# A fused two-block layer on one core, under another table of priorities for the orders of its engines

## The chip, the cores and the metric

The kernel runs on one core of one Trainium2 chip. The metric is the device time of one execution in microseconds, from launch to the last output in memory; the less, the better.

## What is computed

An input x of 2 x 1024 x 128 goes through four residual steps, each on the layer norm of x:

```python
x = x + attn_a(layernorm(x))   # three 128x128 projections, a linear recurrence over 1024 tokens, norm, projection
x = x + ffn(layernorm(x))      # 8 experts, all of them for every token, weighed
x = x + attn_b(layernorm(x))   # three MLPs, low-rank gates, a recurrence on an 8x8 state in each of 16 heads, norm, MLP
x = x + ffn(layernorm(x))      # the same 8 experts again
```

The feed-forward step is the bulk of the work:

```python
g = einsum('bsh,ehf->ebsf', x, w_gate)       # 8 experts, 128 -> 512
u = einsum('bsh,ehf->ebsf', x, w_up)
h = silu(g) * u
expert_out = einsum('ebsf,efh->ebsh', h, w_down)
out = einsum('ebsh,bse->bsh', expert_out, cw)  # cw: product of two softmaxes, normalised
```

The recurrence of attn_b, for each token and head, has an 8x8 state `wkv`, a decay d, a normalised key, a value and a receptance:

```python
tmp = einsum('bhj,bhjk->bhk', a * knt, wkv)
wkv = d[..., None] * wkv - knt[..., None] * tmp[:, :, None, :] + vt[..., None] * rk[:, :, None, :]
out = einsum('bhij,bhj->bhi', wkv, rt)
```

## The kernel before, in words

**Tiles.** The 2048 tokens stand as 16 steps (t = 0 to 15) of 128 tokens. A token's place in a step is a chunk of the sequence, so that each of 128 partitions carries a piece of the sequence through 16 consecutive steps; t = 0 to 7 is the first unit, 8 to 15 the second. Four steps make a block j = 0 to 3 (512 tokens, one 128x512 tile). A feed-forward pass q works on one block: q = 0 to 3 is the first feed-forward step on blocks 0 to 3, q = 4 to 7 the second.

**The experts.** A pass has 32 chunks (8 experts x 4 slices of 128 hidden units), 256 chunks in all, named by m = 0 to 255. Of each, TensorE makes `gate` and `up` (three 128x512 matmuls each, with weights and activations split in a high and a low part), ScalarE the silu (L1140), VectorE the product `hidden` (L1860: `sh_buf<-sh_buf,bank`), and TensorE `down` in two halves of two 128x128 matmuls (each is two records in the trace). After four chunks an expert's sum stands in PSUM. It is added to x either by VectorE, in four instructions that read PSUM (L2159, task `add` where `ADDS[e]` is 1), or by ScalarE, which weighs it (L1253), and GpSimd, which adds it (L1024).

**The steps of attn_b.** For each t of a unit but its first, VectorE makes two products, T1 (L1959, for the transition matrix) and W1 (L1971, for the local state). Each is summed over one index: by TensorE with eight 128x128 matmuls against an identity (tasks T2 and W2, in the trace `bank<-work,ident`, 16 records), where the list `PE_SUMS` has a 1, and otherwise by one VectorE reduction (L1962 for T2). ScalarE copies TensorE's T2 (L1192), GpSimd makes the update of the transition (T3 L974, T4 L984), the outer product (L966) and the product for the output (`readout`, L992); VectorE does W3, W4, W5 (L2001, L2010, L2013) on the local state and `read` (L1950), the reduction of `readout`. After a unit, 64 small products on TensorE (`link`) join the pieces of the sequence, and then per block come `y0` (L2114 and L2116 on VectorE), `through` (L1014 on GpSimd), `y1` (L2122), a norm and an MLP (`back_z`, `back_hidden`, `back_out`, and `back_add`, L2148, on VectorE). Only then can the block's second feed-forward pass begin: `ffn_stats`, `ffn_norm` (L1714), `ffn_z` (transposes on TensorE, a copy on ScalarE), `ffn_low` (L1871).

**What sets the order.** Nothing is reordered while the kernel runs: every engine goes through its own list, and waits on semaphores. The lists are made when the program is written, by a list scheduler (`Plan`) over all tasks of all engines. It picks, among the tasks of an engine that could start within `NEAR` of the first, the one with the highest rank (the length of the path behind it by weights in `WEIGHT`) plus a hand-set lead:

```python
def pick(self, engine):
    ...
    near = min(found)[0] + NEAR
    return max((self.ops[k].rank + self.lead(self.ops[k]) + self.stick(k), -begin, k) for soon, begin, k in found if soon <= near)
```

The leads stand in `LEAD`: one number for each expert slot's group of chunks, for each block's front, steps and back, and for the two chains of links. A number in these tables costs nothing by itself; it moves tasks in the lists. The task names of the lists are used below with their number: hidden.78, T2.7 (step t = 7), y0.2.1 (block 2, second step).

## Time and profile before

| | us |
|---|---|
| runs of the kernel before | 882.91, 886.38, and one of 2961.72 |
| median of the three | 886.38 |
| the profiled execution, its own time | 885.59 |
| its span, first to last instruction | 883.6 |

The profile is of one execution, and rows below count from the start of its span. The span is 2.0 us shorter than that execution's own time. Of the three runs the one of 2961.72 is more than three times the others; the other two are 3.5 us apart. The granted clock is a share of full speed: 1.00 is 2.4 GHz, 0.50 is 1.2 GHz.

### The profile page before, as it was taken

The page shows a single profiled execution, that of the slowest core. Times are in us where ns is not written, and L with a number is a line of the kernel's source. Part 1 is how long each engine was busy: PE and PEld are TensorE (multiplying, and loading weights), DVE is VectorE, ACT ScalarE, POOL GpSimd, SP SyncE. Part 2 cuts the span into 40 slices and gives each one's busy share as a digit, 9 for nine tenths or more (in the row PEclk, how much of TensorE's full clock was granted, in tenths as well). Part 3 has the DMA queues.
Part 4 walks back from the last instruction along what each step waited for, and adds up shares of the span by engine and source line. Part 5 has one row for each costly group of instructions (what it writes and reads, how often), then busy time and mean ns, then how long its engine had stood idle before and what let it go on. Part 6 is the DMA issues. An engine that isn't in the chain of part 4 may idle for free.

```text
span 883.6 us, 14240 instructions
## 1 busy us (share of the span) xinstructions
PE 845.0 (96%) x5342; PEld 728.3 (82%) x5342; DVE 564.9 (64%) x1056; ACT 376.1 (43%) x795; POOL 370.3 (42%) x268
## 2 busy tenths in 40 slices
PE   7999999999999899999999989999999999999997
PEld 5987987888778779897786768988998788878887
DVE  6688553798648981149699987885226789353433
ACT  5253246623682233346646625333233433444332
POOL 4443210297206865445334952786543332100000
PEclk9999999999999999999999999999999999999999
DMA  9500000011001110022110111110003311000000
GB/s 285 120 1 1 1 1 1 25 48 49 24 1 49 49 48 1 1 96 96 49 49 24 48 49 49 49 49 25 13 24 120 96 28 34 1 1 8 6 1 13
DMA packets 20989, 36.03 MB, mean 41 GB/s; under 512 B 3089, under 2 KB 9913, under 8 KB 20921
## 3 DMA queue, kind: packets, MB, share of 16 engines
q1 hardware_dynamic: 20920, 35.13, 12.1%
q8 instruction: 43, 0.70, 0.3%
q14 instruction: 26, 0.21, 0.1%
HBM read 21.49 MB, written 13.63 MB: 40 GB/s over the span
## 4 chain that ended last, share of the span: by engine, by line
PE 39%; DVE 10%; POOL 2%; issue 2%; ACT 0%; DVEq 0%; POOLq 0%; ACTq 0%
PE bank L1316 38%; DVE sh_buf L1860 1%; DVE w_a L2116 1%; DVE states L2114 1%; DVE normed L1714 1%; DVE state L2013 1%; DVE work L1959 1%; POOL readout L992 1%; POOL state L984 1%; DVE bank L2010 0%; POOL work L974 0%; DVE scr L2122 0%; DVE normed L1709 0%; POOL work L966 0%; PE bank L1342 0%
## 5 line engine op out<-in xcount | busy, mean ns | idle before, releaser
L1860 DVE TENSOR_TENSOR sh_buf<-sh_buf,bank 128x512 f32<-128x512 f32 x256 | 172.2, 683 | 220.2 <-PE bank L1316 195.3
L1316 PEld LDWEIGHTS bank<-w_down,sh_buf 128*128 128x128 f32 x2048 | 266.8, 192 | 42.0 <-DVE sh_buf L1860 21.7
L1316 PE MATMUL bank<-w_down,sh_buf 128*128 128x128 f32 x2048 | 286.8, 279 | 11.8 <-DVE sh_buf L1860 11.3
L1140 ACT ACTIVATE sh_buf<-bank 128x512 f32<-128x512 f32 x256 | 152.4, 598 | 279.1 <-PE bank L1316 233.4
L1316 PE MATMUL bank<-z_hi,w_lo 128*128 128x512 f32 x512 | 226.5, 442 | 2.0 <-DVE bank L2001 1.5
L1316 PE MATMUL bank<-z_lo,w_hi 128*128 128x512 f32 x512 | 201.9, 394 | 0.0
L1316 PE MATMUL bank<-z_hi,w_hi 128*128 128x512 f32 x512 | 201.8, 394 | 0.0
L1024 POOL TENSOR_TENSOR x<-x,y_weighted 128x512 f32<-128x512 f32 x43 | 57.5, 1336 | 223.7 <-ACT y_weighted L1253 223.6
L1316 PEld LDWEIGHTS bank<-z_lo,w_hi 128*128 128x128 f32 x512 | 96.2, 188 | 22.7 <-DVE z_lo L1871 0.4
L1316 PEld LDWEIGHTS bank<-z_hi,w_lo 128*128 128x128 f32 x512 | 97.6, 191 | 14.5 <-issue 1.9
L1316 PEld LDWEIGHTS bank<-z_hi,w_hi 128*128 128x128 f32 x512 | 97.3, 190 | 10.1 <-issue 0.2
L1004 POOL TENSOR_TENSOR backs<-backs,head_mask 128x512 f32<-128x512 f32 x64 | 69.3, 1086 | 58.6 <-PE bank L1316 55.4
L1316 PEld LDWEIGHTS bank<-states,backs 128*128 128x128 f32 x508 | 71.6, 191 | 8.5 <-issue 1.9
L1316 PE MATMUL bank<-states,backs 128*128 128x8 f32 x508 | 66.4, 239 | 0.0
L1014 POOL TENSOR_TENSOR backs<-backs,w_a 128x1024 f32<-128x1024 f32 x16 | 42.7, 2682 | 54.8 <-DVE w_a L2116 42.9
L1316 PEld LDWEIGHTS bank<-work,ident 128*128 128x128 f32 x416 | 50.0, 197 | 11.8 <-DVE work L1959 8.4
L1316 PE MATMUL bank<-work,ident 128*128 128x128 f32 x416 | 52.1, 283 | 7.3 <-DVE work L1959 4.1
L1253 ACT ACTIVATE y_weighted<-bank,cw 128x128 f32<-128x128 f32 x172 | 49.4, 369 | 18.6 <-PE bank L1316 18.3
L1221 ACT ACTIVATE states<-bank 128x16 f32<-128x16 f32 x126 | 23.0, 182 | 72.5 <-PE bank L1316 72.4
L966 POOL TENSOR_TENSOR work<-quad,rkv 128x1024 f32<-128x1024 f32 x16 | 31.3, 1954 | 48.4 <-DVE quad L1935 30.8
L992 POOL TENSOR_TENSOR readout<-state,rkv 128x1024 f32<-128x1024 f32 x16 | 40.0, 2502 | 2.8 <-DVE quad L1950 2.8
L984 POOL TENSOR_TENSOR state<-state,work 128x1024 f32<-128x1024 f32 x16 | 39.0, 2435 | 0.7
(227 smaller groups left out, 955.6 us busy)
## 6 DMA issues: line engine op xcount, KB each, us to landing
trans_spill<-state SPq DMA_DIRECT2D x16, 512.0 KB, 2.6
backs<-trans_spill SPq DMA_DIRECT2D x16, 512.0 KB, 3.3
backs<-keep_spill SPq DMA_DIRECT2D x4, 1024.0 KB, 5.5
x<-in_x SPq DMA_DIRECT2D x4, 256.0 KB, 5.9
backs<-in_w_gate SPq DMA_DIRECT2D x4, 256.0 KB, 5.2
backs<-in_w_up SPq DMA_DIRECT2D x4, 256.0 KB, 5.4
keep_spill<-rkv SPq DMA_DIRECT2D x4, 256.0 KB, 2.5
keep_spill<-low SPq DMA_DIRECT2D x4, 256.0 KB, 2.6
```

The source lines that it names most:

```text
L966: pool.tensor_tensor(outer.rearrange("p (h i k) -> p h i k", h=H, i=N), vs[:, i, :].rearrange("p (h i) -> p h i", h=H).unsqueeze(3).broadc ...
L984: pool.tensor_tensor(trans, trans, prod_t, ALU.subtract).then_inc(S["trans_rdy"], 1)
L992: pool.tensor_tensor(readout[:].rearrange("p (h i k) -> p h i k", h=H, i=N), locst.rearrange("p (h i k) -> p h i k", h=H, i=N), over_i(rec ...
L1004: pool.tensor_tensor(blocks_d[:, p % RING].rearrange("p c b (h i) -> p (c b) h i", h=H), src.unsqueeze(2).broadcast_to((P, PIECE * B, H, N ...
L1014: pool.tensor_tensor(t_ring[t % 2].rearrange("p (h i j) -> p h i j", h=H, i=N), t_ring[t % 2].rearrange("p (h i j) -> p h i j", h=H, i=N), ...
L1024: pool.tensor_tensor(flat(x[:, G * j:G * j + G, :]), flat(x[:, G * j:G * j + G, :]), y_weighted[:], ALU.add).then_inc(S["x_added"], 1)
L1140: act.activation(s_buf[:, m % 2, :], bank_of("gate", m)[:], ACT.Silu).then_inc(S["silu_done"], 1)
L1221: act.activation(dst, bank_of("links", u)[:, first:first + B * N].rearrange("p (b k) -> p b k", b=B), ACT.Copy).then_inc(S["link_rdy"], 1)
L1253: ins = act.activation(y_weighted[:, i * P:(i + 1) * P], bank_of("y", eg)[:, i * P:(i + 1) * P], ACT.Identity, scale=cw[:, q % 2, i, e:e + 1])
L1316: return pe.matmul(dst, lhs, rhs, start=start, stop=stop, **kw)
L1714: return dve.tensor_tensor(normed[:, n % 2], normed[:, n % 2], per_tile(rstd[:, n % 2, :]), ALU.mult)
L1860: dve.tensor_tensor(h_buf[:, m % 4, :], s_buf[:, m % 2, :], bank_of("up", m)[:], ALU.mult).then_inc(S["h_done"], 1)
```

## The change

Five tables get new numbers. No instruction is written otherwise, and no function is touched.

```diff
-PE_SUMS = dict(T2=[1, 1, 1, 1, 1, 1, 0, 1, 0, 1, 1, 1, 1, 1, 1, 1], W2=[0, 0, 1, 1, 1, 1, 1, 1, 1, 1, 1, 1, 1, 1, 1, 1])
+PE_SUMS = dict(T2=[0, 1, 1, 1, 1, 1, 0, 0, 0, 1, 1, 1, 1, 1, 1, 1], W2=[0, 0, 1, 1, 1, 1, 1, 1, 1, 1, 1, 1, 1, 1, 1, 1])
-WEIGHT = dict(pe=1.83, act=1.30, dve=1.42, pool=1.48, sp=1.64)
+WEIGHT = dict(pe=1.83, act=1.30, dve=1.44, pool=1.48, sp=1.53)
```

`PE_SUMS`: the sum T2 of step 7 goes from TensorE to VectorE (eight 128x128 matmuls and one ScalarE copy out, one reduction L1962 in). Step 0 has no such sum, so its new 0 does nothing. `ADDS` (64 entries): the experts that VectorE adds rise from 21 to 28. New on VectorE are numbers 3, 5, 22, 27, 33, 37, 41, 44, 45, 48, 56 and 62; back to ScalarE and GpSimd go 38, 40, 47, 53 and 57. `LEAD` has 42 of its 64 expert numbers changed, and four others. With `WEIGHT` and `LEAD` the lists change. TensorE's list keeps every matmul but those of T2.7. Over 256 chunks, the gates and ups stand in most places as before; the changes of kind in TensorE's list between a gate or up and a down rise from 383 to 397 (down to gate or up: 198 to 208; gate or up to down: 185 to 189). ScalarE's list has one switch of its function table fewer, 42 for 43.

**Place 1, VectorE, steps 6 and 7** (T1 L1959, T2 L1962, W1 L1971, read L1950, W3 L2001, hidden L1860). Before:

```order
L2013 TENSOR_TENSOR state<-state,bank 128x512
L1959 TENSOR_TENSOR work<-state,bank 128x1024
L1962 TENSOR_REDUCE tmp<-work 128x128
L1971 TENSOR_TENSOR work<-state,bank 128x1024
L1950 TENSOR_REDUCE quad<-readout 128x128
L1860 TENSOR_TENSOR sh_buf<-sh_buf,bank 128x512
L2001 TENSOR_TENSOR bank<-quad,bank 128x512
L2010 TENSOR_TENSOR bank<-work,bank 128x512
L1959 TENSOR_TENSOR work<-state,bank 128x1024
L1860 TENSOR_TENSOR sh_buf<-sh_buf,bank 128x512 x2
L2013 TENSOR_TENSOR state<-state,bank 128x512
```

Now:

```order
L2013 TENSOR_TENSOR state<-state,bank 128x512
L1959 TENSOR_TENSOR work<-state,bank 128x1024
L1971 TENSOR_TENSOR work<-state,bank 128x1024
L1962 TENSOR_REDUCE tmp<-work 128x128
L1950 TENSOR_REDUCE quad<-readout 128x128
L2001 TENSOR_TENSOR bank<-quad,bank 128x512
L2010 TENSOR_TENSOR bank<-work,bank 128x512
L1860 TENSOR_TENSOR sh_buf<-sh_buf,bank 128x512 x3
L2013 TENSOR_TENSOR state<-state,bank 128x512
L2001 TENSOR_TENSOR bank<-quad,bank 128x512
L2010 TENSOR_TENSOR bank<-work,bank 128x512
```

W1.6 stands ahead of the reduction T2.6 and W3.6 behind it without a hidden between, and three hiddens follow together. In step 7 the new reduction stands in the same way behind W1.7. On TensorE the sum W2.6 still follows up.79; T2.7 is gone, and W2.7 goes from behind up.81 to ahead of it.

**Place 2, VectorE, steps 10 and 11 with the front of block 3** (z_lo<-bank,z_hi L1871 is ffn_low.5; L1714 is ffn_norm.5). Before, from the end of W4.10 on:

```order
L2010 TENSOR_TENSOR bank<-work,bank 128x512
L2013 TENSOR_TENSOR state<-state,bank 128x512
L1959 TENSOR_TENSOR work<-state,bank 128x1024
L1971 TENSOR_TENSOR work<-state,bank 128x1024
L1950 TENSOR_REDUCE quad<-readout 128x128
L1860 TENSOR_TENSOR sh_buf<-sh_buf,bank 128x512 x2
L2001 TENSOR_TENSOR bank<-quad,bank 128x512
L2010 TENSOR_TENSOR bank<-work,bank 128x512
L1860 TENSOR_TENSOR sh_buf<-sh_buf,bank 128x512
L2013 TENSOR_TENSOR state<-state,bank 128x512
L2001 TENSOR_TENSOR bank<-quad,bank 128x512
L2010 TENSOR_TENSOR bank<-work,bank 128x512
```

Now:

```order
L2010 TENSOR_TENSOR bank<-work,bank 128x512
L2013 TENSOR_TENSOR state<-state,bank 128x512
L1871 TENSOR_TENSOR z_lo<-bank,z_hi 128x512
L1860 TENSOR_TENSOR sh_buf<-sh_buf,bank 128x512
L1959 TENSOR_TENSOR work<-state,bank 128x1024
L1971 TENSOR_TENSOR work<-state,bank 128x1024
L1860 TENSOR_TENSOR sh_buf<-sh_buf,bank 128x512 x2
L1950 TENSOR_REDUCE quad<-readout 128x128
L2001 TENSOR_TENSOR bank<-quad,bank 128x512
L2010 TENSOR_TENSOR bank<-work,bank 128x512
L2013 TENSOR_TENSOR state<-state,bank 128x512
```

The pair T1.11 and W1.11 (L1959, L1971), which stood ahead of hidden.131, now stands behind it, hidden.132 and hidden.133 and read.10 come between that pair and W3.11, and ffn_low.5 comes ahead of it all. On TensorE, T2.11 and W2.11 go from behind up.133 to behind gate.134. Just before this place, T1.9, ffn_stats.5, front_norm.3 and W3.9 go ahead of hidden.128: there VectorE has between hidden.127 and hidden.128 now ffn_low.4, W5.8, W1.9, back_add.1, front_stats.3, logits.4, front_centre.3, T1.9, ffn_stats.5, front_norm.3 and W3.9, where it had the first five. TensorE's T2.9 and its transposes front_z.3 go ahead of down.128. A little later (chunks 139 to 142) the small matmuls route.5 go from behind up.141 to directly ahead of T2.12.

**Place 3, VectorE, the back of block 2** (chunks 172 to 178: y0 L2114 and L2116, y1 L2122, add L2159). Before:

```order
L2114 TENSOR_TENSOR states<-w_sb,backs 128x1024
L2116 TENSOR_REDUCE w_a<-states 128x128
L2114 TENSOR_TENSOR states<-w_sb,backs 128x1024
L2116 TENSOR_REDUCE w_a<-states 128x128
L1860 TENSOR_TENSOR sh_buf<-sh_buf,bank 128x512 x3
L2122 TENSOR_REDUCE scr<-backs 128x128
L1860 TENSOR_TENSOR sh_buf<-sh_buf,bank 128x512
L2122 TENSOR_REDUCE scr<-backs 128x128
L2114 TENSOR_TENSOR states<-w_sb,backs 128x1024
L2116 TENSOR_REDUCE w_a<-states 128x128
```

Now:

```order
L2114 TENSOR_TENSOR states<-w_sb,backs 128x1024
L2116 TENSOR_REDUCE w_a<-states 128x128
L1860 TENSOR_TENSOR sh_buf<-sh_buf,bank 128x512 x2
L2114 TENSOR_TENSOR states<-w_sb,backs 128x1024
L2116 TENSOR_REDUCE w_a<-states 128x128
L1860 TENSOR_TENSOR sh_buf<-sh_buf,bank 128x512
L2122 TENSOR_REDUCE scr<-backs 128x128
L1860 TENSOR_TENSOR sh_buf<-sh_buf,bank 128x512
L2122 TENSOR_REDUCE scr<-backs 128x128
L1860 TENSOR_TENSOR sh_buf<-sh_buf,bank 128x512
L2114 TENSOR_TENSOR states<-w_sb,backs 128x1024
L2116 TENSOR_REDUCE w_a<-states 128x128
```

A hidden stands behind nearly every single y0 or y1, where two y0 stood together. The tail of this block moves later for it: back_add.2 and ffn_stats.6 go from behind hidden.185 to behind hidden.189, ffn_norm.6 from behind hidden.187 to behind hidden.190, and ffn_z.6 on TensorE from behind down.186 to between down.190 and down.191. The next gate, gate.192, is the first that needs it. VectorE's y0.3.0 stands between hidden.191 and ffn_low.6, which gate.192 also needs.

## Rows read from the trace of the kernel before

**Rows 1.** Part 1 of the page: each engine's busy time, share of the span, instructions.

```profile
PE 845.0 (96%) x5342; PEld 728.3 (82%) x5342; DVE 564.9 (64%) x1056; ACT 376.1 (43%) x795; POOL 370.3 (42%) x268
```

**Rows 2.** Busy time by stretch: length, then PE, PEld, DVE, ACT, POOL busy.

```profile
core 0: us, PE busy (x) PEld busy (x) DVE busy (x) ACT busy (x) POOL busy (x), PEclk, DMA share, GB/s
0.00:44.20 44.20, 38.57 (x236) 32.73 (x237) 29.36 (x87) 18.62 (x36) 20.07 (x35) 1.00 0.72 202
...
265.10:309.30 44.20, 40.51 (x278) 36.17 (x278) 39.30 (x52) 10.81 (x27) 33.76 (x17) 1.00 0.13 49
...
441.80:486.00 44.20, 41.79 (x247) 34.06 (x246) 41.44 (x80) 23.93 (x42) 17.25 (x13) 0.96 0.12 37
486.00:530.20 44.20, 39.14 (x234) 32.44 (x233) 39.88 (x68) 20.88 (x38) 34.05 (x17) 0.96 0.12 48
...
662.70:706.90 44.20, 40.94 (x261) 33.66 (x260) 31.09 (x47) 17.58 (x33) 15.64 (x8) 1.00 0.33 108
```

**Rows 3.** Waits of PE: released by whom, total, times, longest.

```profile
PE bank L1316 <- DVE sh_buf L1860: 12.4, 13, 2.1
...
PE bank L1316 <- DVE work L1959: 4.1, 4, 2.0
```

**Rows 4.** Groups of the page: busy and mean ns, then idle before.

```profile
L1860 DVE TENSOR_TENSOR sh_buf<-sh_buf,bank 128x512 f32<-128x512 f32 x256 | 172.2, 683 | 220.2 <-PE bank L1316 195.3
...
L1024 POOL TENSOR_TENSOR x<-x,y_weighted 128x512 f32<-128x512 f32 x43 | 57.5, 1336 | 223.7 <-ACT y_weighted L1253 223.6
```

**Rows 5.** Timeline of PE around steps 6 and 7: start, length.

```profile
288.44 1.05 PE L1316 MATMUL bank<-w_down,sh_buf 128*128 128x128 f32 x8
289.25 0.48 PE L1316 MATMUL bank<-z_hi,w_lo 128*128 128x512 f32 x1
...
290.04 0.39 PE L1316 MATMUL bank<-z_hi,w_lo 128*128 128x512 f32 x1
...
290.73 0.39 PE L1316 MATMUL bank<-z_hi,w_lo 128*128 128x512 f32 x1
...
293.72 2.05 PE L1316 MATMUL bank<-work,ident 128*128 128x128 f32 x16 [2.13 <-DVE work L1971]
...
299.10 2.02 PE L1316 MATMUL bank<-work,ident 128*128 128x128 f32 x16 [1.04 <-DVE sh_buf L1860]
300.96 0.28 PE L1316 MATMUL bank<-w_down,sh_buf 128*128 128x128 f32 x1
```

**Rows 6.** Timeline of DVE at the same place.

```profile
290.43 2.11 DVE L1962 TENSOR_REDUCE tmp<-work 128x128 f32<-128x1024 f32 x1
```

**Rows 7.** Timeline of DVE, steps 9 to 11 and after.

```profile
501.16 2.33 DVE L1921 TENSOR_TENSOR quad<-quad,bs 128x512 f32<-128x512 f32 x1
...
520.25 0.69 DVE L2001 TENSOR_TENSOR bank<-quad,bank 128x512 f32<-128x512 f32 x1 [1.88 <-PE bank L1316]
...
523.14 0.69 DVE L2013 TENSOR_TENSOR state<-state,bank 128x512 f32<-128x512 f32 x1 [0.88 <-POOL readout L992]
...
539.55 0.69 DVE L1860 TENSOR_TENSOR sh_buf<-sh_buf,bank 128x512 f32<-128x512 f32 x1 [5.71 <-PE bank L1316]
```

**Rows 8.** Timeline of DVE in the back of block 2.

```profile
683.08 1.22 DVE L2114 TENSOR_TENSOR states<-w_sb,backs 128x1024 f32<-128x1024 f32 x1
684.34 1.22 DVE L2116 TENSOR_REDUCE w_a<-states 128x128 f32<-128x1024 f32 x1
...
687.61 1.12 DVE L2159 SCALAR_TENSOR_TENSOR x<-bank,cw,x 128x128 f32<-128x128 f32 x4
```

**Rows 9.** Timeline of PE at the same place.

```profile
675.31 1.16 PE L1316 MATMUL bank<-w_down,sh_buf 128*128 128x128 f32 x8 [0.94 <-DVE sh_buf L1860]
...
686.34 1.16 PE L1316 MATMUL bank<-w_down,sh_buf 128*128 128x128 f32 x8 [1.63 <-DVE sh_buf L1860]
```

**Rows 10.** Timeline of PE at T2.12 and W2.12.

```profile
550.03 2.16 PE L1316 MATMUL bank<-work,ident 128*128 128x128 f32 x17 [1.35 <-DVE work L1959]
```

**Rows 11.** Busy time of one stretch, as in rows 2; clock after POOL.

```profile
511.00:517.00 6.00, 4.01 (x18) 3.34 (x17) 5.72 (x9) 0.00 (x0) 1.95 (x1) 0.81 0.00 1
```

More of the change, by code:

```diff
@@ L77 @@
 CHUNK_TIME = 2.50
-WEIGHT = dict(pe=1.83, act=1.30, dve=1.42, pool=1.48, sp=1.64)
-LEAD = dict(experts=[11.2, -87.7, -100.8, -18.6, -7.1, 1.4, -5.6, 3.6, -40.4, -8.9, -37.3, -76.4, 53.6, 156.3, 44.0, 14.3, -13.0, -10.5, -58.7, -80.1, 115.0, -61.5, 186.2, 9.8, 131.0, -34.9, 143.6, -139.3, -103.2, -5.8, -70.5, 19.9, 109.7, 56.6, -153.6, -112.2, -93.4, -79.7, 25.3, -4.3, -85.7, 94.2, -98.8, -42.4, 5.9, -19.9, -0.0, 38.4, -87.0, 157.1, -98.7, 265.2, -112.3, -83.8, -173.8, 149.0, 110.0, 2.9, -60.1, -144.7, -109.6, 121.9, -151.0, 159.5], front=[-66.9, -115.2, -46.1, 54.6], steps=[25.1, 36.8, -35.8, -2.2], back=[17.3, 83.9, 4.9, 3.0], chain=[-5.6, 76.6], other=[57.7])
+WEIGHT = dict(pe=1.83, act=1.30, dve=1.44, pool=1.48, sp=1.53)
+LEAD = dict(experts=[4.2, -87.7, -88.0, -18.6, -22.3, 12.1, -5.6, -90.5, -54.7, 64.5, -23.7, -76.4, -25.5, 113.4, 47.5, 0.5, 4.9, -10.5, 104.3, -88.8, 233.7, 66.6, 186.2, 9.8, 136.6, -34.9, 143.6, -143.2, -21.7, -5.8, -70.5, 16.3, 107.0, 52.2, -156.6, -29.5, -93.4, -79.7, 22.2, 15.0, -85.7, -9.1, -85.5, -36.7, -4.4, -9.9, -43.9, 38.4, -84.4, 157.1, -98.7, 265.2, -112.3, -129.9, -232.2, 147.7, 188.1, 2.2, -60.1, -144.7, -107.0, 121.9, -178.6, 167.5], front=[-66.9, -115.2, -46.1, 54.6], steps=[25.1, 14.0, -35.8, -2.2], back=[-3.1, 83.9, 4.9, 15.0], chain=[-5.6, 67.5], other=[57.7])
 NEAR = 0.21
```

2 lines of the change are left out of this document (1 added, 1 removed).

## The prediction

> **What bounds the kernel now.** I read the page's busy shares first. TensorE is busy for 845.0 of the span's 883.6 us, 96%, and no other engine for more than 64% [rows 1]. So the time is TensorE's work plus the 38.6 us in which it stands still, and a change of order can act on those alone, apart from what it does to the work itself. The second view is busy time in twenty stretches of 44.2 us; a stretch's idle time is its length less TensorE's busy time [rows 2]. The first stretch has 5.6 us: loads and the first weights, which both orders go through in the same way. Then the idle time gathers where VectorE is nearly full: 3.7 us in 265 to 309 (VectorE 39.3 of 44.2), 2.4 us in 442 to 486 (41.4) and 5.1 us in 486 to 530 (39.9); and 3.3 us in 663 to 707, where VectorE's 31.1 us are in lumps. The waits of TensorE say the same by name: 12.4 us for `hidden` in 13 waits, and 4.1 us for the products T1 and W1 in 4 [rows 3]. The reader is to see in this a fixed work on TensorE, held up by a VectorE that is late at a few places because something long stands ahead of what TensorE needs. Each place can be looked up in both orders.
>
> **TensorE's own work.** T2.7 goes. Its eight matmuls run from 299.10 to the next down at 300.96, so 1.9 us less [rows 5]. Against it, the kind of work changes more often. The first gate after a down starts at 289.25 and the up at 290.04, 0.79 us; the up takes until 290.73, 0.69 us, and it came after a gate [rows 5]. A change from down to gate or up costs some 0.1 us, by these rows; the order has 10 more of those and 4 more the other way, for which I take the same. That is 14 x 0.09 = 1.3 us more. Net **-0.6 us**; ends -1.9 (the changes cost nothing) and +0.2 (0.15 each). The Trainium skill (TensorE: Matmul & The Clock Gate, Back-to-back issue gap) gives for a warm stream a gap of N/2.4 + 2.5 ns, 216 ns at 512 columns, which knows nothing of what the neighbour is. By that rule the term would be -1.9, and the sum below 1.3 us lower. The row disagrees, since equal matmuls differ by their neighbour, and I go by the row.
>
> **Steps 6 and 7 (place 1).** TensorE waits 2.13 us for W1.6 and 1.04 us for what stands ahead of T2.7 [rows 5]. W1.6 is late because the reduction T2.6 of 2.11 us stands ahead of it [rows 6]. Now W1.6 goes first, so the first wait loses its cause, and T2.7's wait goes with T2.7. 3.2 us are to be had. Against them VectorE gets a second such reduction, 2.1 us, in a stretch where it is 89% busy, and three hiddens stand together behind W3.6, whose own wait for TensorE's sum is covered by T2.6 and `read`. I take off a quarter and keep **-2.4 us**; ends -3.2, and +1 if the reduction is paid in full once more.
>
> **Steps 9 to 11 (place 2).** Of VectorE's 4.3 us of idle time in 486 to 530 [rows 2], 1.88 us end at 520.25, a wait for TensorE's W2.11, and 0.88 us at 523.14, a wait for `readout`; only at 539.55 has it air, 5.71 us [rows 7]. While it is full, TensorE's idle time is set by VectorE's total, whatever the order inside; what the order can save is VectorE's own waits. Now hidden.132, hidden.133 (0.7 us each, [rows 4]) and `read` (1.2 us, as the reduction L2116 of the same size [rows 8]) stand between the pair T1.11, W1.11 and W3.11. They cover a sum of 1.9 us on TensorE and the wait of 1.88 with it. ffn_low.5 comes in from the airy side, 0.7 us, and costs a part of that. **-2.0 us**, ends -2.8 and 0. Just ahead, hidden.128 now stands behind six more VectorE tasks, some 5.5 us: T1.9 1.2, and for the others 0.7 us for each pass over a 128x512 tile [rows 4], six such passes, and logits.4 with next to nothing. TensorE has T2.9 and front_z.3 (1.9 and 0.5 us) and the gates, which it had anyway, to pass the time; but T2.9 and front_z.3 themselves wait for T1.9 and front_norm.3 in that queue. I step through it with single durations: down.128 is reached about 1.3 us before its hidden. **+1.3 us**, ends 0 and +3. If VectorE is full anyway, this is partly the same idle time seen earlier, so I count it as a cost only once.
>
> **T2.12.** It waits 1.35 us [rows 10]. The small matmuls route.5, 0.8 us, move into that wait: **-0.8 us**, ends -0.8 and 0.
>
> **The back of block 2 (place 3).** A y0 is 1.22 + 1.22 = 2.4 us of VectorE [rows 8]. Two of them in a row, 4.9 us, made the next hidden late by 0.94 us at 675.31 and by 1.63 us at 686.34 [rows 9]. TensorE's chunk is 2.3 us: gate 0.79, up 0.69, and down 0.81, from 288.44 to 289.25 [rows 5]; a single y0 and a hidden are 3.1 us, so each y0 makes VectorE late by 0.8 us, and the next chunk with an y1 or nothing makes it up. I expect 2.6 us of waits to shrink to 0.5: **-2.1 us**, ends -2.6 and 0. But the block's tail comes some four chunks later, and now ends at the pass: ffn_z.6 stands between down.190 and down.191, and gate.192 needs ffn_low.6, ahead of which VectorE has y0.3.0. From the end of up.191: hidden.191 0.7, y0.3.0 2.4, ffn_low.6 0.7, together 3.9; TensorE in the meantime down.190 0.8, ffn_z.6 0.5, down.191 0.8 and two matmuls of gate.192 0.5, together 2.6. **+1.3 us** of a new wait; ends 0 and +2.5.
>
> **The adds.** Seven experts more go to VectorE at 1.12 us each [rows 8], 7.9 us in all; ScalarE loses 7 x 4 weighings, GpSimd 7 x 1.34 = 9.4 us [rows 4]. Neither of the two bounds a stretch, so nothing is gained there directly. On VectorE most of the new ones stand where it is half idle (numbers 41, 44 to 48, 56, 62) or has the 5.7 us of air (33). Number 27 stands behind back_norm.0, in the fullest part of pass 3. **+0.5 us**, ends 0 and +3. Of the ports, first the row: L1921 takes 2.33 us at 501.16 [rows 7], while a product of the same size takes 0.68 [rows 4], in a stretch in which GpSimd is busy for 34.1 of 44.2 us [rows 2]. The Trainium skill (SBUF — State Buffer, SBUF: two separate sides) has a VectorE operation with two SBUF inputs and a GpSimd operation exclude each other for their whole length, and an add out of PSUM has one SBUF input. By that rule 9.4 us less of GpSimd would also free VectorE's own operations where it is full; since only numbers 27 and 33 are near those places, the sum would be at most some 1 us lower.
>
> **Sum.** -0.6 - 2.4 - 2.0 + 1.3 - 0.8 - 2.1 + 1.3 + 0.5 = -4.8 us. From the profiled execution: span 883.6 - 4.8 = 878.8, and its own time 2.0 us more, 880.8. The median of the runs shown, 886.38, is 0.8 above the profiled time; from it, 881.6. I forecast between the two, **881.0 us**, 0.6% less.
>
> **The rivals.**
> *More is gained: the clock pieces go too.* The granted clock falls to 0.81 in 511 to 517 us [rows 11], which is a piece at 1.2 GHz right behind TensorE's waits for VectorE; the mean of 0.96 in two stretches of 44.2 us [rows 2] is (1 - 0.96) x 44.2 / 0.5 = 3.5 us at the lower level in each. At half speed each costs up to 1.7 us. If the shorter waits of place 2 spare both, and the costs that I added for hidden.128 and gate.192 don't come, the sum is -4.8 - 2.6 - 3.4 = -10.8: 875.0 us. For it speaks that the piece in 511 to 517 follows the waits that are to go; against, that hiddens 123 to 127 ahead of the first piece stand as before.
> *Nothing changes.* VectorE's total in its full stretches is the same or more, and TensorE only waits elsewhere. Then just TensorE's own -0.6 and half of place 3 remain, and the new waits take them: 885.5 us. For it: idle time lies where VectorE is 89 to 94% busy. Against: place 3, where it is not.
> *Slower: VectorE's added work is paid where it is full.* One mechanism: T2.7 (2.1 us) and add 27 (1.1 us) come in full, each hidden behind them is late by that, and the lumps ahead of hidden.128 and gate.192 cost their upper ends (3 and 2.5 us), while place 3 still gives 2.1 and T2.7's own 1.9 are saved against 1.3 of changes. 2.1 + 1.1 + 3 + 2.5 - 2.1 - 0.6 = +6.0: 891.5 us. It decides when VectorE's queue at hidden.128 is more than some 4 us behind TensorE; there the gates ahead no longer cover it.
> *The change does not do what it says* can be ruled out by the orders: the lists differ on all five queues.
>
> **How the numbers follow.** Forecast (877.5 to 884): 0.47. More gained (868 to 877.5): 0.20. Nothing changes (884 to 887.5): 0.18. Slower: 0.15. The range leaves out half of the last and a tenth at the low end: **872.5 to 888.5**. About 2% is what a measurement of this kernel can tell from no change, 868.7 and 904.1 us. TensorE's work of 845.0 us and the fixed start and end bound the gain: 17.7 us of 38.6 would have to go, more than half of the middle's idle time, and only the rival above comes near. Faster by over 2%: 0.04; within: 0.94; slower by over 2%: 0.02.
>
> **What would show it.** In the profile of the changed kernel: 112 instructions of L2159 for 84, and two of L1962 for one. The sum W2.6 begins without a wait over 0.5 us; no wait of TensorE over 1 us for hiddens between chunks 172 and 182; a wait of about 1.3 us at gate.192 for L1871, and of the same size ahead of down.128; VectorE's wait of 1.88 us at W3.11 is gone; TensorE's idle total is 33 to 35 us and its busy time 844 to 845. The prediction is wrong if the idle time stays near 38 with other names, or if the new waits at the two named places exceed 3 us.

## The result, and the profile after

The changed kernel takes **886.27 us** (median of 20 runs, 884.33 to 890.28), the kernel before 885.12 beside it (20 runs, from 882.87): ratio 1.0025, 95% interval [1.0013, 1.0037]. By the ratio that is 2.2 us slower, where 881.0 us, 4.8 less than the profiled execution, was forecast. The time is inside the range, on the other side of no change. Here and below a ratio compares all runs of both kernels, without the one of 2961.72 us; the two medians alone are 1.2 us apart. The profiled execution took 887.32 us.

The page's part 1 of the changed kernel, against [rows 1]:

```profile
PE 845.7 (95%) x5326; PEld 726.8 (82%) x5326; DVE 573.2 (65%) x1085; ACT 367.6 (42%) x765; POOL 360.0 (41%) x261
```

TensorE stands still for 885.6 - 845.7 = 39.9 us (before 38.6). The stretches of [rows 2], in the changed kernel:

```profile
core 0: us, PE busy (x) PEld busy (x) DVE busy (x) ACT busy (x) POOL busy (x), PEclk, DMA share, GB/s
0.00:44.20 44.20, 38.57 (x236) 32.74 (x237) 29.18 (x87) 18.62 (x36) 19.90 (x35) 1.00 0.71 202
44.20:88.40 44.20, 41.96 (x232) 34.29 (x230) 35.52 (x82) 17.13 (x33) 18.56 (x17) 0.96 0.01 1
265.10:309.30 44.20, 36.90 (x250) 32.64 (x249) 39.99 (x51) 13.95 (x30) 30.21 (x16) 1.00 0.13 49
...
486.00:530.20 44.20, 38.84 (x221) 30.50 (x220) 39.81 (x64) 20.63 (x38) 31.05 (x18) 0.92 0.09 37
662.70:706.90 44.20, 44.20 (x297) 39.37 (x296) 34.44 (x58) 14.31 (x30) 12.09 (x7) 1.00 0.33 110
706.90:751.10 44.20, 42.16 (x255) 34.90 (x254) 30.52 (x54) 19.54 (x32) 12.58 (x7) 1.00 0.12 40
```

The same view of the kernel before has two rows for stretches that [rows 2] lacks:

```profile
44.20:88.40 44.20, 43.99 (x257) 36.95 (x255) 36.37 (x85) 19.87 (x40) 18.46 (x18) 1.00 0.00 1
...
706.90:751.10 44.20, 44.20 (x280) 38.84 (x278) 38.71 (x73) 15.91 (x29) 13.89 (x9) 1.00 0.11 31
```

Place 3 gains its 3.3 us (40.94 to 44.20). The second stretch is now idle for 2.2 us, where before it was for 0.2; the prediction never looked at it. The stretch of place 1 is idle for 7.3 us where it was for 3.7, that of place 2 for 5.4 where it was for 5.1, and that of gate.192 for 2.0 where it had no idle time.

The waits of TensorE by name, against [rows 3] (total, times, longest):

```profile
PE bank L1316 <- DVE sh_buf L1860: 11.3, 15, 2.9
...
PE bank L1316 <- DVE bank L2001: 3.3, 1, 3.3
...
PE bank L1316 <- DVE work L1971: 2.8, 2, 1.7
PE bank L1316 <- DVE work L1752: 2.0, 1, 2.0
PE bank L1316 <- DVE z_lo L1871: 1.7, 2, 1.5
...
PE bank L1316 <- DVE work L1959: 1.3, 3, 0.6
```

Set task against task, the start of TensorE's down.m in this trace less that in the trace before is +4.6 us from chunk 40 on, +6.0 at chunk 100, +3.3 at 140, +4.4 at 168 and +1.9 at the end. (These differences are worked out by giving each TensorE record to its task; the two orders also swap neighbours, so only places where both have done the same tasks are used.) The loss is made in the head. Of its 4.6 us, 1.7 is the clock: the granted clock is 0.50 from 60.9 to 64.3 us in this execution and 1.00 there in the one before. Steps 6 and 7 add to the loss at first, but between chunks 100 and 103 (in 380 to 425 us, where TensorE is idle for 0.15 us and before was for 1.96) more than that comes back: +3.2 at chunk 103, 1.7 less than at chunk 70. From there to chunk 144 nothing is gained, then 1.1 is lost, and 2.5 are gained from chunk 168 to the end. The forecast had zero for the head.

The three largest new waits, in TensorE's timeline of the changed kernel: kv.2 in the head, down.77 at place 1, front_hidden.3.4 at place 2.

```profile
60.56 2.63 PE L1316 MATMUL bank<-work,w_a 128*128 128x512 f32 x3 [1.97 <-DVE work L1752]
```

```profile
301.50 1.16 PE L1316 MATMUL bank<-w_down,sh_buf 128*128 128x128 f32 x8 [2.92 <-DVE sh_buf L1860]
```

```profile
501.89 2.93 PE L1316 MATMUL bank<-backs,b_w 128*128 128x512 f32 x3 [3.26 <-DVE bank L2001]
```

### The profile page after: what moved, and what is told of

It is laid out like the page before. It is cut to its first block, busy times and chain, and to the rows that moved or that the text cites. A ratio compares the mean times of both kernels' runs of the same rounds, so it can differ in the third digit from the quotient of the medians.

```text
span 885.6 us, 14205 instructions
## 1 busy us (share of the span) xinstructions
PE 845.7 (95%) x5326; PEld 726.8 (82%) x5326; DVE 573.2 (65%) x1085; ACT 367.6 (42%) x765; POOL 360.0 (41%) x261
## 4 chain that ended last, share of the span: by engine, by line
PE 62%; DVE 14%; POOL 5%; issue 4%; ACT 1%; DVEq 0%; POOLq 0%; ACTq 0%
PE bank L1316 62%; DVE sh_buf L1860 2%; POOL readout L992 1%; POOL state L984 1%; DVE work L1959 1%; DVE bank L1882 1%; DVE state L2013 1%; POOL rstd L948 1%; POOL work L974 1%; POOL work L966 1%; DVE w_a L2116 1%; DVE states L2114 1%; DVE state L2021 1%; DVE work L1971 0%; DVE bank L2010 0%
## 5 line engine op out<-in xcount | busy, mean ns | idle before, releaser
L1860 DVE TENSOR_TENSOR sh_buf<-sh_buf,bank 128x512 f32<-128x512 f32 x256 | 172.5, 683 | 217.0 <-PE bank L1316 198.0
L1024 POOL TENSOR_TENSOR x<-x,y_weighted 128x512 f32<-128x512 f32 x36 | 48.3, 1342 | 199.6 <-ACT y_weighted L1253 199.5
L1316 PEld LDWEIGHTS bank<-work,ident 128*128 128x128 f32 x400 | 47.3, 194 | 7.8 <-DVE work L1971 3.6
L1316 PE MATMUL bank<-work,ident 128*128 128x128 f32 x400 | 49.2, 280 | 4.2 <-DVE work L1971 2.8
L1253 ACT ACTIVATE y_weighted<-bank,cw 128x128 f32<-128x128 f32 x144 | 41.7, 370 | 14.7 <-PE bank L1316 14.7
L2159 DVE SCALAR_TENSOR_TENSOR x<-bank,cw,x 128x128 f32<-128x128 f32 x112 | 31.4, 342 | 19.0 <-PE bank L1316 18.9
L946 POOL TENSOR_SCALAR var_eps<-mean_var 128x4 f32<-128x4 f32 x20 | 9.9, 495 | 76.0 <-DVE mean_var L1700 75.8
```

Of the source, the lines that this page charges most:

```text
L946: step.inc(pool.tensor_scalar(var_eps[:, n % 2, :], mean_var[:, n % 2, :, 1], eps, None, ALU.add))
L1024: pool.tensor_tensor(flat(x[:, G * j:G * j + G, :]), flat(x[:, G * j:G * j + G, :]), y_weighted[:], ALU.add).then_inc(S["x_added"], 1)
L1253: ins = act.activation(y_weighted[:, i * P:(i + 1) * P], bank_of("y", eg)[:, i * P:(i + 1) * P], ACT.Identity, scale=cw[:, q % 2, i, e:e + 1])
L1316: return pe.matmul(dst, lhs, rhs, start=start, stop=stop, **kw)
L1860: dve.tensor_tensor(h_buf[:, m % 4, :], s_buf[:, m % 2, :], bank_of("up", m)[:], ALU.mult).then_inc(S["h_done"], 1)
L2159: ins = dve.scalar_tensor_tensor(out=xt(j)[:, i, :], in0=bank_of("y", eg)[:, i * P:(i + 1) * P], scalar=cw[:, q % 2, i, e:e + 1], in1=xt(j ...
```

## The experiments

Most experiments work in the same way: the kernel takes both orders' lists and splices them at points where both have done the same tasks on every engine, so that one part of the change stands alone. PSUM banks are named anew where the two lists give different ones, and nothing else differs. The edit is then one line with the parts, given here in words; in the kernels they are places in the lists. Every ratio is to the kernel before on the same chip (medians of it 883.6 to 885.3). Line numbers in these kernels are shifted. A figure in us behind a ratio is worked out from the ratio.

### The change in four parts

```diff
-schedule()
+LISTS = dict(before=lists(...), after=lists(...))
+PARTS = [after to hidden.44, before to the end]                            # e1_head
+PARTS = [before to hidden.70, after to hidden.103, before to the end]      # e2_place1
+PARTS = [before to hidden.103, after to hidden.144, before to the end]     # e3_mid
+PARTS = [before to hidden.168, after to the end]                           # e4_tail
```

> The changed lists up to chunk 44 on every engine, the lists of before from there on (experts 3 and 5 added by VectorE). Theory 'place by place': the loss is made by the order in chunks 4 to 18, where in the changed kernel's profile TensorE waits 2.1 us for kv.2 and 1.6 us for down.6; this kernel is 4.6 us slower than before (0.5%), 890. Rival 'VectorE's added work': the loss follows the added work, here 2 adds of 1.1 us in a stretch in which VectorE is 80% busy, so at most 1 to 2 us slower.

> The changed lists between chunk 70 and chunk 103 alone (T2.7 and expert 22 on VectorE), the lists of before on both sides. Place by place: the gain foretold for steps 6 and 7 is not there, the profiles' chunk times say 1.2 us slower than before. Rival 'VectorE's added work': 3.2 us more VectorE work, of it 2.1 us where it is full: 2 us or more slower. The prediction's own term would be 4.3 us faster.

> The changed lists between chunk 103 and chunk 144 alone (experts 27 and 33 on VectorE). Place by place: 2.7 us faster than before (0.3%), about 882.5. Rival 'VectorE's added work': 2 adds in the fullest stretch, not faster, up to 2 us slower.

> The changed lists from chunk 168 to the end (experts 41, 44, 45, 47, 48, 53, 56, 57 and 62 as in the changed kernel, 3 adds more on VectorE than before). Place by place: 2.5 us faster than before (0.3%), the back of block 2 gives 4 and gate.192 takes 1.8 back. Rival 'VectorE's added work': the part with the most added adds, so 1 to 3 us slower.

| part | ratio | interval | us | forecast of this part |
|---|---|---|---|---|
| e1_head | 1.0030 | [1.0016, 1.0044] | +2.7 | 0 |
| e2_place1 | 0.9999 | [0.9984, 1.0014] | -0.1 | -4.3 |
| e3_mid | 1.0013 | [0.9999, 1.0027] | +1.1 | -1.5 |
| e4_tail | 0.9967 | [0.9952, 0.9982] | -2.9 | -0.8 and adds |

The parts sum to +0.8 us, the whole change to +2.2; each part is uncertain by 1.2, and chunks 44 to 70 (+0.3 us in the trace) and 144 to 168 (+1.1) are in none. The tail is faster than both kernels though it holds three of the seven added experts. So added work on VectorE does not make a kernel slower wherever it stands; but here VectorE is less full (34.4 and 30.5 of 44.2 us in the last two stretches above), and the forecast's rival had it paid where it is full. The adds were changed alone in no run. The head is the largest loss. It came out at 2.7 us and not at the 4.6 of the trace, because e1_head's profile (+2.9 at chunk 44) has no lower clock at 60.9 us.

### The tail: gate.192's wait

```diff
+MOVES = [('dve', ('y0', 3, 0), 'behind', ('ffn_low', 6))]
```

> The new order from chunk 168 on, as in e4_tail (ratio 0.9967, 881.1 us), and in it VectorE's y0.3.0 moved from ahead of ffn_low.6 to behind it. Place by place: TensorE's wait of some 1.5 to 1.8 us at gate.192 for ffn_low.6 goes, because ffn_low.6 begins 2.4 us earlier, and the time falls by 1.0 to 1.8 us against e4_tail, to about 879.6 us, ratio 0.995. Rival, the wait only moves: y0.3.0 now stands ahead of hidden.192, which comes late by as much, and the time is that of e4_tail within 0.5 us.

Measured: 880.44 us, ratio 0.9956 [0.9940, 0.9973], 0.001 below e4_tail. TensorE's wait of 1.48 us for `z_lo` (L1871) at gate.192 is gone from its timeline. From chunk 168 to the end the trace of e4_tail gains 2.1 us on that of the kernel before, and that of m1_tail_low 3.6, both at full clock there: 1.5 us for the move. The intervals of the two runs overlap, so the size stands on two profiles; the wait's disappearance is shown.

### The head: first the tasks, then the two engines

```diff
+MOVES = [('dve', ('hidden', 6), 'ahead', ('mix', 2)), ('pe', ('kv', 2), 'behind', ('gate', 9))]   # m2_head_hidden
+MOVES = [('pool', ('ffn_stats', 1), 'behind', ('split', 9))]                                      # n1_head_split
```

> The new order up to chunk 44, as in e1_head (887.8 us, ratio 1.003), with hidden.6 ahead of mix.2 on VectorE and kv.2 behind gate.9 on TensorE. In the new order's profile TensorE waits 2.14 us at kv.2 for mix.2 and 1.56 us at down.6 for hidden.6, near 57.7 and 60.6 us. Place by place: these two waits make the larger part of the head's loss of 3 to 4.6 us; with them gone or halved the time falls by 2 to 3 us against e1_head, to 885 or 886 us, ratio 1.000 to 1.001. Rival, the head loses by the sum of VectorE's work up to there and by the pieces of lower clock: each engine is late as before, some other task waits, and the time stays within 1 us of e1_head.

Measured: 887.56 us, ratio 1.0039 [1.0025, 1.0053]. The waits at kv.2 and down.6 became one of 1.1 us at kv.2 and one of 1.6 at the transposes ffn_z.1. Rearranging the tasks that wait does not remove the cause. It shows in VectorE's and GpSimd's timelines of the changed kernel:

```profile
55.77 0.68 DVE L1747 TENSOR_TENSOR work<-state 128x512 f32<-128x512 f32 x1
56.49 4.01 DVE L1752 SCALAR_TENSOR_TENSOR work<-work,cols,state 128x512 f32<-128x512 f32 x3
```

```profile
56.06 3.23 POOL L1039 TENSOR_TENSOR w_lo<-backs,w_hi 128x512 fp32r<-128x512 f32 x2
```

The same in the kernel before, where only the end of the L1752 meets the pair of L1039:

```profile
63.10 2.08 DVE L1752 SCALAR_TENSOR_TENSOR work<-work,cols,state 128x512 f32<-128x512 f32 x3
```

```profile
64.74 3.26 POOL L1039 TENSOR_TENSOR w_lo<-backs,w_hi 128x512 fp32r<-128x512 f32 x2 [1.83 <-PE bank L1316]
```

In the changed kernel the three L1752 of `mix`.2 lie on the pair: 1.7 us each for the first two in place of 0.75, and 4.0 in all. Taken one by one, GpSimd's two end at 57.61 and 59.29 us, and the two stretched L1752 at 58.15 and 59.84, each 0.5 us behind: VectorE's instruction gets ahead only when GpSimd's has ended.

> The new order up to chunk 44, as in e1_head (ratio 1.003), with one task of GpSimd moved: ffn_stats.1 goes from ahead of split.8 and split.9 (the subtractions L1039 that split the weights) to behind them, where the old order has it. In e1_head two of VectorE's three instructions of mix.2 (L1752) take 1.67 and 1.76 us in place of 0.75, exactly while GpSimd runs the two L1039 at 56.0 to 59.2 us, and TensorE waits 2.14 us at kv.2 for them. Theory, contention of the two engines at this place: the splits run some 2 us earlier, at 53.8, mix.2 takes 2.1 to 3 us in place of 4.0, the waits at kv.2 and down.6 lose 1 to 2 us, and the time is 1.5 to 2.5 us below e1_head's, ratio 1.0005 to 1.0015. Rival, the order of VectorE itself costs the time (mix.2 ahead of hidden.6, combine.0 ahead of both): the waits and the ratio stay as in e1_head, 1.003.

Measured: 888.45 us, ratio 1.0050 [1.0035, 1.0065]; the expectation missed, and the run separates nothing. GpSimd's pair still began at 55.8, since it waits for a gate that TensorE makes; L1747 was stretched to 1.7 us and the L1752 took 2.98.

So the collision was taken away with a wait, and no list was touched:

```diff
                     elif i >= 6:
                         pool.wait_ge(S["g_full"], i // 2 * FC - 8)
+                        if i == 8:
+                            pool.wait_ge(S["mixed_rdy"], 3)
```

> e1_head (the new order up to chunk 44) with one wait added on GpSimd: split.8 also waits for mix.2, so that the two L1039 run behind VectorE's three L1752 and not beside them. No order is changed. Contention: the three L1752 take 2.1 to 2.3 us in place of 4.0, TensorE's wait at kv.2 falls from 2.1 to some 0.3 us and hidden.6 is 1.7 us earlier; the head's loss falls by 1.5 to 2 us or more: ratio 1.0005 to 1.0015. Rival, VectorE's own order: mix.2 takes about as long as before or hidden.6 is late all the same, and the ratio stays at 1.003 to 1.005 as in e1_head and n1_head_split.

Measured: 885.72 us, ratio **1.0011** [0.9999, 1.0022], against 1.0030 of e1_head. VectorE's and GpSimd's timelines of h1_split_waits (L2514 is L1752, L1801 is L1039):

```profile
56.46 2.08 DVE L2514 SCALAR_TENSOR_TENSOR work<-work,cols,state 128x512 f32<-128x512 f32 x3
58.45 0.68 DVE L2622 TENSOR_TENSOR sh_buf<-sh_buf,bank 128x512 f32<-128x512 f32 x1
```

```profile
64.40 2.84 POOL L1801 TENSOR_TENSOR w_lo<-backs,w_hi 128x512 fp32r<-128x512 f32 x2 [8.35 <-issue]
```

The pair begins at 64.4, behind mix.3 and not, as the expectation has it, behind mix.2: the semaphore counts from mix.1, since step 0 has no mix, so its third is mix.3. It keeps the pair clear of both. The three L1752 take 2.08 us again, TensorE's wait of 2.0 us at kv.2 and that at down.6 are gone from its timeline, and the head's loss in the trace falls from 2.9 to 1.1 us, with the clock at 1.00 in the head of both. So some two thirds of the head's loss are the two engines in each other's way. The intervals of the two ratios overlap; the size stands on the traces. The rest, about 1 us, stays unexplained.

### Place 1: the sum and the order apart

```diff
+MOVES = [('dve', ('hidden', 77), 'ahead', ('W3', 6)), ('dve', ('hidden', 80), 'ahead', ('W3', 7))]   # m3_place1_hidden
```

> The new order from chunk 70 to 103 (steps 6 and 7), as in e2_place1 (885.0 us, ratio 0.9999), with hidden.77 ahead of W3.6 and hidden.80 ahead of W3.7 on VectorE, as the old order has them relative to W3. Place by place: TensorE's wait of 3.27 us at down.77 and of 1.01 us at down.80 came of these hiddens standing behind a task that itself waits for TensorE's sum W2; the first shrinks below 1 us, the second below 0.5, and the time falls by 2 to 3 us against e2_place1, to 882 to 883 us, ratio 0.997 to 0.998. Rival, VectorE's total in that stretch sets the time (T2.7's reduction of 2.1 us more): down.77 is on time, but W4.6, T1.7 and W1.7 come later by as much, and the time stays within 0.7 us of e2_place1.

Measured: 884.43 us, ratio 0.9997 [0.9981, 1.0013], no better than e2_place1. The rival held: the wait at down.77 shrank and W2.7 got what it lost, by TensorE's timeline:

```profile
295.28 1.16 PE L1774 MATMUL bank<-w_down,sh_buf 128*128 128x128 f32 x8 [1.59 <-DVE sh_buf L2318]
...
303.34 1.83 PE L1774 MATMUL bank<-work,ident 128*128 128x128 f32 x14 [2.69 <-DVE work L2429]
```

Then the two halves of the change at this place by themselves. The sum alone, in the old lists:

```diff
+ORDER["pe"].remove(("T2", 7))
+ORDER["act"].remove(("T2", 7))
+ORDER["dve"].insert(ORDER["dve"].index(("W1", 7)) + 1, ("T2", 7))
```

> The order before, with one thing changed: the sum T2.7 is made by VectorE behind W1.7 (one reduction, 2.1 us) and not by TensorE (1.9 us) and ScalarE's copy. Theory, VectorE's total sets the time in this stretch: TensorE's 1.9 us and its wait of 1.2 us ahead of T2.7 go, but hidden.80 and W3.7 come 2.1 us later, so that 0 to 1 us of the 3.1 is kept: ratio 0.999 to 1.000. Rival, place by place as in the prediction: 3.1 us go and at most 0.5 comes back, ratio 0.997.

Measured: 890.71 us, ratio **1.0082** [1.0067, 1.0096]: 7.2 us slower, far outside both. GpSimd's T3.7 and then TensorE's finish_T.0.0 in its timelines:

```profile
305.59 1.95 POOL L979 TENSOR_TENSOR work<-quad,tmp 128x1024 f32<-128x1024 f32 x1 [6.30 <-DVE tmp L1967]
```

```profile
317.08 1.33 PE L1545 MATMUL bank<-ident,backs 128*128 128x128 f32 x5 [4.26 <-DVE backs L2098]
```

and in those of the kernel before:

```profile
301.51 1.96 POOL L974 TENSOR_TENSOR work<-quad,tmp 128x1024 f32<-128x1024 f32 x1 [2.17 <-ACT tmp L1192]
```

```profile
313.01 1.09 PE L1540 MATMUL bank<-ident,backs 128*128 128x128 f32 x8 [0.97 <-DVE backs L2093]
```

What counts is not VectorE's 2.1 us but when the sum is ready: GpSimd gets it 4.1 us later, and its chain T3.7, T4.7 carries this to the end of the unit, where TensorE waits 4.3 us. Right behind this wait the granted clock is 0.50 for 6.8 us (315.7 to 322.5), where the kernel before has 1.00; at half speed that is up to 3.4 us more. It is no accident of this profile: the six executions of n2_t27_alone have a mean granted clock of 0.9922, those of the kernel before beside them 0.9955; at half speed that makes up to 2.9 us (0.0033 x 884). So some 4 of the 7.2 us are waits for the late sum, and the rest goes with the clock behind them.

The order alone, e2_place1 with the sum back on TensorE:

```diff
+ORDER["dve"].remove(("T2", 7))
+ORDER["pe"].insert(ORDER["pe"].index(("W2", 7)), ("T2", 7))
+ORDER["act"].insert(ORDER["act"].index(("silu", 81)) + 1, ("T2", 7))
+BANK["sum_t", 7] = "U0"
```

> e2_place1 (the new order from chunk 70 to 103, ratio 0.9999) with the sum T2.7 back on TensorE, ahead of W2.7, and its copy on ScalarE behind silu.81: the new order alone, where n2_t27_alone had the changed sum alone (ratio 1.008). If the two parts add, the order alone would gain 7 us, ratio 0.992. If the new order only repairs what the sum on VectorE breaks (GpSimd's T3.7 waits for it, and the end of the unit's recurrence for that), it gives nothing itself: ratio 0.999 to 1.001. By the prediction's terms it would be 1.3 us slower than e2_place1, since TensorE gets its 1.9 us back and VectorE loses 2.1: 1.001.

Measured: 886.70 us, ratio 1.0020 [1.0007, 1.0033]. Order alone +1.8 us, sum alone +7.2, both together -0.1. They don't add: the new order repairs most of what the sum breaks (its GpSimd list has outer.7 and add.19 ahead of T3.7, in the wait for the sum), and costs by itself.

### The middle: bonus.2

```diff
+MOVES = [('dve', ('bonus', 2), 'behind', ('W5', 9))]        # m4_mid_bonus
+MOVES = [('dve', ('bonus', 2), 'behind', ('hidden', 136))]  # k1_bonus_late
```

> The new order from chunk 103 to 144 (steps 9 to 11), as in e3_mid (886.5 us, ratio 1.0013), with VectorE's bonus.2 moved from ahead of W4.9 to behind W5.9. The matmul front_hidden.3.4 takes the PSUM bank that the sum W2.9 holds until W4.9 has read it, and TensorE waits 3.4 us for that at 498 us. Place by place: with bonus.2 out of the way W4.9 comes some 1 to 2 us earlier, the wait shrinks to about 2 us, and the time falls by 1 to 2 us against e3_mid, to about 885 us, ratio 1.000. Rival, VectorE is full in this stretch, and bonus.2 delays the next hidden instead, so the time stays within 0.5 us of e3_mid.

Measured: 884.87 us, ratio 1.0002 [0.9989, 1.0015], 1.0 us below e3_mid by the ratios. The wait for the bank is gone, and one of 2.77 us stands at W2.10 in its place. What had been in the way is plain in VectorE's and GpSimd's timelines of the changed kernel. bonus.2 is the first four rows:

```profile
493.55 1.65 DVE L1915 TENSOR_TENSOR quad<-rkv 128x512 f32<-128x512 f32 x1
495.24 0.69 DVE L1917 TENSOR_REDUCE bs<-quad 128x64 f32<-128x512 f32 x1
495.96 1.60 DVE L1919 TENSOR_TENSOR quad<-rkv,rows 128x512 f32<-128x512 f32 x1
497.60 2.72 DVE L1921 TENSOR_TENSOR quad<-quad,bs 128x512 f32<-128x512 f32 x1
```

```profile
494.61 2.40 POOL L974 TENSOR_TENSOR work<-quad,tmp 128x1024 f32<-128x1024 f32 x1
497.09 2.67 POOL L984 TENSOR_TENSOR state<-state,work 128x1024 f32<-128x1024 f32 x1
```

The three products take 5.97 us in place of 3 x 0.69, while GpSimd runs without a gap; the reduction between them, with one input, is not stretched. W4.9 stands behind, and frees the bank.

> The new order from chunk 103 to 144, as in e3_mid (ratio 1.0013), with VectorE's bonus.2 moved from ahead of W4.9 to behind hidden.136. Nothing but block_end.2, behind it, needs it. In the new order's profile its four instructions take 6.7 us at 493.5 to 500.3, beside GpSimd's T3 and T4, where four of 0.69 us would take 2.8, and TensorE waits 3.3 us right behind them for a PSUM bank that W4.9 frees. Contention in a full stretch: 2.8 us of work and 3.9 us of stretching leave the queue ahead of W4.9, the wait of 3.3 us shrinks below 1 us, and the time falls by 3 to 5 us against e3_mid: ratio 0.996 to 0.998. Rival: whatever stands there in place of bonus.2 is stretched or late in the same way (m4_mid_bonus only moved the wait behind up.130), and the sum of VectorE's work up to chunk 136 sets the time: ratio 0.9995 to 1.0015.

Measured: 880.74 us, ratio **0.9956** [0.9943, 0.9970], 5 us below e3_mid. VectorE's timeline of k1_bonus_late:

```profile
524.57 1.08 DVE L2321 TENSOR_TENSOR quad<-rkv 128x512 f32<-128x512 f32 x1
525.69 0.69 DVE L2323 TENSOR_REDUCE bs<-quad 128x64 f32<-128x512 f32 x1
526.41 0.69 DVE L2325 TENSOR_TENSOR quad<-rkv,rows 128x512 f32<-128x512 f32 x1
527.13 0.69 DVE L2327 TENSOR_TENSOR quad<-quad,bs 128x512 f32<-128x512 f32 x1
```

It takes 3.2 us there, and of TensorE's waits at front_hidden.3.4 and W2.10 only 0.4 us is left. The middle of the new order is better than the old one by 3.9 us once this task is out of it.

Not all of that is the waits. The profile of the kernel before has two pieces at a clock of 0.50 in the middle (473.8 and 514.7 us, 3.4 us each), that of e3_mid one, that of k1_bonus_late none. From chunk 103 to 144 the trace of k1_bonus_late gains 5.5 us on that of the kernel before; the two pieces are 3.4 of these, and 2.1 are left. The executions say the same: four of the six of k1_bonus_late have a mean clock of 0.998 or 0.999, while none of 134 of the kernel before is above 0.997. Executions with an equal mean clock of 0.998 are 884.4 and 884.6 us (e3_mid) and 880.7 and 880.8 us (k1_bonus_late), so 3.8 of the 5 us between these two are not the clock.

> m1_tail_low (old order to chunk 168, new from there, y0.3.0 behind ffn_low.6; ratio 0.9956) with the old order's bonus.2 moved behind hidden.136 as well. In the old order it takes 4.4 us at 499.0 to 503.4 ahead of hidden.130, and TensorE waits 0.75, 1.6, 2.2 and 1.7 us at 506 to 515. If VectorE's load ahead of these waits sets them, 2 to 4 us go: ratio 0.992 to 0.994, 877 to 878 us. Rival: the waits hang on the steps' chain over TensorE and GpSimd and not on VectorE's load: 0.995 to 0.9965.

Measured: 882.79 us, ratio 0.9980 [0.9969, 0.9991], worse than m1_tail_low without the move. In the old order TensorE still waits 2.0 us ahead of T2.11, and bonus.2 now begins at 528 us, stretched once more (1.66 us for its last product). By hidden.138 the trace is 2.5 us ahead of the kernel before, and by hidden.139 only 0.3: VectorE waits 2.7 us there for ScalarE's `rkv`, and TensorE then 2.0 us for hidden.139, at 545.8, with one more piece at the lower clock. The mean clock of the twelve executions is 0.994, against 0.995 for the kernel before and for m1_tail_low, so about 1 us of what is lost goes with the clock. So the gain of k1_bonus_late is not the move as such; it needs the new order around it. Which task of that order it is was not tested.

### Together

> The whole new order with three tasks moved: GpSimd's ffn_stats.1 behind split.9, VectorE's bonus.2 behind W5.9, VectorE's y0.3.0 behind ffn_low.6. If the three places add up, it is 1.5 to 2.5 (head) + 0 to 1 (bonus) + 0.8 to 1.5 (y0) = 2.3 to 5 us below the new order: 881.5 to 884 us, ratio 0.997 to 0.9995. Rival, the places don't add, since the pieces of lower clock and later waits take the time back: ratio 1.000 to 1.0025.

Measured: 883.88 us, ratio 1.0000 [0.9986, 1.0014], 2.2 us below the changed kernel by the ratios: hardly the least gain that the sum of the places gave, and the rival's value as well. The run does not decide between them. Its move in the head is that of n1_head_split, which had gained nothing.

> The whole new order with three repairs of the causes found: split.8 waits for mix.2 (head), bonus.2 behind hidden.136 (middle), y0.3.0 behind ffn_low.6 (tail). If the three places add: 1.0025 - 0.002 to 0.003 (head) - 0.002 to 0.004 (middle) - 0.001 (tail) = ratio 0.9945 to 0.9975, 879 to 882 us. Rival: place 1 and the remaining order keep the loss, and the places take from each other: 0.999 to 1.001.

Measured: **878.39 us**, ratio 0.9923 [0.9909, 0.9937], 9 us below the changed kernel by the ratios. In the trace it is at +0.9 us after the head (changed kernel +4.6), -5.7 at chunk 140 (+3.3) and -8.6 at the end (+1.9). Its middle is at full clock, where the profiles of both other kernels have two pieces at half speed: 3.4 us of the fall. One wait of GpSimd (the same as in h1_split_waits) and two moves on VectorE turn the change from a loss into a gain.

> The old order up to chunk 103, the new one from 103 to 144 with bonus.2 behind W5.9, the old one to 168, the new one from there with y0.3.0 behind ffn_low.6. Sum of m1_tail_low (-3.9 us by ratio) and m4_mid_bonus (+0.2): ratio 0.9955 to 0.996, 880 us. Rival, the middle part gains its 0.8 us of the profile too: 0.9945.

Measured: 881.03 us, ratio 0.9968 [0.9956, 0.9979]. That is no better than m1_tail_low alone (0.9956), and inside the intervals no worse: the middle with bonus.2 as in m4_mid_bonus adds nothing that can be seen.

> The old order to chunk 103 (head and place 1), the new one from 103 to 144 with bonus.2 behind hidden.136, the old one to 168, the new one from there with y0.3.0 behind ffn_low.6: the two parts that gain, mended, and neither that loses. If the parts add: 0.9956 (k1_bonus_late) x 0.9956 (m1_tail_low) = 0.991, some 877 us, 1 us below k3_after_mended2. Rival: they take from each other, or the new order's adds and T2.7 in the head and place 1, once mended, gain something after all: 0.9925 to 0.994.

Measured: **876.56 us**, ratio 0.9915 [0.9900, 0.9931], 7.5 us faster than before by the ratio (8.7 by the medians of 5 and 9 runs), and the lowest of all; the two parts multiply to 0.9912, so they add. Its page:

```profile
PE 842.6 (96%) x5342; PEld 726.9 (83%) x5342; DVE 567.2 (65%) x1076; ACT 369.6 (42%) x774; POOL 359.7 (41%) x263
```

TensorE stands still for 874.8 - 842.6 = 32.2 us, 6.4 less than before. The mean clock of its five executions is 0.998, that of the nine of the kernel before beside them 0.995, so up to 2.9 us of the 7.5 go with the clock, and the other 4.6 do not. k3_after_mended2 has 0.9923, inside the intervals; in its trace it loses 1.0 us in the head and 1.1 between chunks 144 and 168, where z_best has the old order, and gains 1.4 at place 1.

## Why the prediction was wrong

**The step that failed first: "loads and the first weights, which both orders go through in the same way".** True to 44 us, and the prediction then looked only at the stretches where the old kernel was idle. The second stretch had 0.2 us of idle time, so no place in it was compared; the change put 2.7 us there. An order can lose where the old one has nothing to lose. The other three parts came to -1.9 us by their ratios, and the whole without the head's 2.7 to -0.5; so the head turned the sign, and the size was wrong without it too. By parts, the measured time less the forecast is 2.7 us in the head, 4.2 at steps 6 and 7, 2.6 in the middle and -2.1 in the tail. The clock has a share in it: the 20 executions of the changed kernel have a mean of 0.9940, 134 of the kernel before 0.9952, and at half speed the difference is about 1 us (0.0012 x 886). The sum had no term for the clock; only a rival had.

**Steps 6 and 7, forecast -2.4 and T2.7's -1.9: measured together -0.1.** The wait for W1.6 did go, as foretold (W2.6 begins without one). But three hiddens behind W3.6 wait for TensorE's sum and then come late: 2.92 us at down.77. The prediction called W3.6's wait covered and did not ask who waits behind it. Between chunks 100 and 103, which it did not look at, some of this comes back. And it priced T2.7 by the time it takes on VectorE, not by when GpSimd gets it; alone it costs 7.2 us. The upper end given, "+1 if the reduction is paid in full once more", was too small for that mechanism. With the sum back on TensorE in the new order the ratio is 0.0021 higher, 1.9 us; that is the net of T2.7's matmuls, its reduction and the waits of both, and the intervals overlap, so the 1.9 us for the matmuls themselves is not tested.

**Steps 9 to 11, forecast -1.5 with hidden.128 and T2.12: measured +1.1 (interval -0.1 to +2.4).** TensorE's wait for hidden.128 came out at 0.3 us (1.3 forecast). What was missed is bonus.2. The prediction read its L1921 at 2.33 us [rows 7] and named the cause, but weighed it for the adds alone: "the sum would be at most some 1 us lower". The Trainium skill (SBUF — State Buffer, SBUF: two separate sides) has a VectorE instruction with two SBUF inputs and a GpSimd one that reads SBUF exclude each other for the whole instruction; the trace agrees, with L1752 ending 0.5 us behind each of GpSimd's two (0.75 us when free), and so do h1_split_waits and k1_bonus_late. What matters is which instructions an order lays side by side: 1.9 us longer for `mix`.2 in the head, and 3.9 us longer for bonus.2, ahead of TensorE's largest new wait.

**The back of block 2: right in the mechanism, too small.** -2.1 forecast and 3.3 us in the stretch. **gate.192's +1.3: right**, 1.48 us waited for L1871, and gone in m1_tail_low; by two profiles all of it counts, 1.5 us. **T2.12 with route.5**: its wait is gone from the list (longest for L1959 now 0.6 us). **The changes of kind**: z_best has 11 more than before, as many matmuls, and 2.4 us less busy time, with two pieces at 1.2 GHz (1.7 us each) fewer. That leaves 1.0 us for the 11, the 0.09 us forecast; it is one pair of profiles, not a test of its own.

**The rivals.** Slower came true in sign, not shown in its mechanism: e4_tail and k3_after_mended2, the latter with all 28 experts on VectorE, are faster than the kernel before, but no run had the new order with the old adds. Its T2.7 term was the right suspect with the wrong price. "More is gained" describes k3_after_mended2 and z_best, the clock pieces that go with the waits included, not this change.
